# Third stage of an adaLN block: the gated residual by transpositions of VectorE's columns instead of products with diagonals

## The reference

```python
h = _layernorm(x) * (1 + ca) + sa
x = x + ga * _L1_attn_ref(h, ...)          # the change is here
# _L1_attn_ref, one step from a zero state:
xi = x @ W_in.T                            # x is h here
nr = B_real * xi ; ni = B_imag * xi        # the old state is zero
y  = sum(C_real * nr - C_imag * ni)        # so y is xi times a constant per feature
out = y @ W_out.T
return h + _rmsnorm(out, norm_w)           # the residual is h, so ga * h is needed too
```

## Time and profile before

| | us |
| --- | --- |
| three runs | 1878.19, 1873.54, 1880.81 (median 1878.19) |
| profiled execution | 1875.54 |
| its span | 1873.8 |
| stage C, first product to the first of stage D | 1237.61 to 1317.89 |
| `back`, last expert product to the first of stage C | 1205.6 to 1237.6 |

### The profile page before, as it was taken

One profiled execution on the slowest core, in us unless ns is written; L12 is line 12 of the kernel. 1 busy time (PEld: TensorE's weight loads), 2 busy tenths in 40 slices (PEclk: granted clock), 3 DMA queues, 4 the chain that ended last, 5 costly groups with the idle time before them and its releaser, 6 DMA issues.

```text
span 1873.8 us, 25682 instructions
## 1 busy us (share of the span) xinstructions
PE 1787.5 (95%) x8308; PEld 1401.4 (75%) x8308; DVE 1173.4 (63%) x2140; ACT 757.9 (40%) x1478; POOL 723.7 (39%) x698
## 2 busy tenths in 40 slices
PE   8889999999999999998898998979999999999998
PEld 5567878788878888876666776658778788787886
DVE  5557666676666766676754443557646657567476
ACT  2544555555454555534532222356632222213211
POOL 1433121211222211264344456635455536436342
PEclk9999999999999999999899999989999999999999
DMA  6101454535462544632368999730011001001001
GB/s 253 68 8 35 147 169 135 152 87 187 112 200 69 174 140 146 186 105 92 113 226 253 282 286 282 163 118 18 28 35 51 12 29 51 29 10 56 7 29 73
DMA packets 99955, 216.35 MB, mean 115 GB/s; under 512 B 8504, under 2 KB 33096, under 8 KB 98336
## 3 DMA queue, kind: packets, MB, share of 16 engines
q1 hardware_dynamic: 77744, 166.60, 28.1%
q0 software_dynamic: 11520, 28.96, 6.4%
q10 hardware_dynamic: 10608, 19.74, 3.2%
HBM read 123.93 MB, written 91.35 MB: 115 GB/s over the span
## 4 chain that ended last, share of the span: by engine, by line
PE 73%; DVE 9%; DMA 6%; issue 5%; POOL 3%; ACT 3%; POOLq 0%; ACTq 0%; DVEq 0%; SPq 0%
PE bank L810 21%; PE bank L812 20%; PE bank L811 20%; DMA u_d<-yt,sm 5%; PE bank L1051 3%; PE bank L1217 2%; PE bank L997 2%; PE bank L914 1%; DVE hh L2345 1%; DVE rr L2009 1%; PE bank L1058 1%; POOL gbt L2601 1%; PE bank L999 1%; POOL mark L2612 1%; PE bank L884 1%
## 5 line engine op out<-in xcount | busy, mean ns | idle before, releaser
L2009 DVE RECIPROCAL rr<-rr 128x256 f32<-128x256 f32 x128 | 218.8, 1730 | 0.0
L2444 POOL TENSOR_TENSOR x<-x,tmp 128x512 f32<-128x512 f32 x76 | 116.2, 1533 | 258.8 <-DVE tmp L2002 258.8
L810 PE MATMUL bank<-W1a,hT 128*128 128x512 f32 x512 | 209.4, 409 | 3.4 <-DVE hT L1931 3.4
L810 PE MATMUL bank<-hT,W1b 128*128 128x512 f32 x512 | 208.8, 408 | 2.4 <-DVE hh L2302 2.4
L811 PE MATMUL bank<-hT,W1b 128*128 128x512 f32 x512 | 204.0, 398 | 0.0
L812 PE MATMUL bank<-hT,W1b 128*128 128x512 f32 x512 | 203.8, 398 | 0.0
L812 PE MATMUL bank<-W1a,hT 128*128 128x512 f32 x512 | 201.1, 393 | 0.0
L811 PE MATMUL bank<-W1a,hT 128*128 128x512 f32 x512 | 200.3, 391 | 0.0
L2302 DVE TENSOR_TENSOR hh<-hh,bank 128x512 f32<-128x512 f32 x64 | 43.8, 688 | 183.4 <-PE bank L812 146.7
L2369 POOL TENSOR_TENSOR W<-stage,W 128x1024 fp32r<-128x1024 f32 x32 | 77.2, 2412 | 184.4 <-ACT W L1300 182.1
L2034 DVE SCALAR_TENSOR_TENSOR kt<-bank,kt 128x256 fp32r<-128x256 f32 x128 | 50.5, 395 | 152.8 <-ACT vt L1439 152.6
(11 more groups left out here) (299 smaller groups left out, 4555.3 us busy)
## 6 DMA issues: line engine op xcount, KB each, us to landing
hs_d<-bor SPq DMA_DIRECT2D x24, 1548.0 KB, 12.0
ws_d<-W SPq DMA_DIRECT2D x48, 512.0 KB, 6.1
WB<-ws_d SPq DMA_DIRECT2D x8, 3072.0 KB
stage<-wa SPq DMA_DIRECT2D x32, 512.0 KB, 5.5
stage<-wbe SPq DMA_DIRECT2D x24, 512.0 KB, 4.2
stage<-wdn SPq DMA_DIRECT2D x24, 512.0 KB, 3.9
hg<-hs_d ACTq DMA_DIRECT2D x39, 258.0 KB
mw<-wmod SPq DMA_DIRECT2D x5, 1024.0 KB, 5.0
```

The lines of the kernel that those rows point to most:

```text
L810: pe.matmul(o, lhs(HI), rhs(HI), start=start, stop=False, **kw)
L2009: dve.reciprocal(rr[:, pair, h], rr[:, pair, h]).then_inc(r_rec, 1)
L2444: pool.tensor_tensor(xt, xt, tmp[:, (key + t) % 2, :], ALU.add).then_inc(ring_done, 1)
```

## The change

The diagonals are gone. DVE multiplies each chunk in `tmp` by its gate, feature by feature, while the features still lie on partitions (`gated_columns`, 16 instructions, into `gh`, which takes the place of `dg`). PE then turns the four chunks of a tile by four transpositions (fp32, 128x128) at the end of the tile, and the result goes to x as before. The wait for the bank of this result moves from the tile's start to its end. ACT may write a chunk into `tmp` only when DVE has read the chunk two before it. The rows of layernorm (2, 1) are scaled by DVE (`normed_rows`) and not by ACT, ahead of the statistics of (2, 2). `normed` of a batch runs for all four tiles before the first `gated` of the next.

```diff
-        def over_diag(a):
-            return a("before_dg", [P, 8208]), a("dg", [P, NB, 2, NC, P], F32R)
+        def over_gated(a):
+            return a("before_gh", [P, 8208]), a("gh", [P, 2, NC, S])
@@ PE, step_c
-                pe.wait_ge(dg_lo, NC * (b + 1))
...
-                    if n < 2:
-                        pe.wait_ge(ring_read, ln_at(2, 0, 2 + (n + RING[("ln", 2, 0, 1)]) % 2) + 1)
-                    else:
-                        pe.wait_ge(res_read, n - 1)
...
-                            gated = pe.matmul(o[:, c * P:(c + 1) * P], h(wl), dg[:, b, wr, c, :],
-                                              start=at_ends[0], stop=at_ends[1], skip_group_check=True)
                         if c == NC - 1:
                             product.then_inc(y_full, 1)
+                            if n < 2:
+                                pe.wait_ge(ring_read, ln_at(2, 0, 2 + (n + RING[("ln", 2, 0, 1)]) % 2) + 1)
+                            else:
+                                pe.wait_ge(res_read, n - 1)
+                            for i in range(NC):
+                                if t == 0:
+                                    pe.wait_ge(gh_done, NC * b + i + 1)
+                                gated = pe.transpose(o[:, i * P:(i + 1) * P], gh[:, b % 2, i, t * P:(t + 1) * P], ident[:, :])
                             gated.then_inc(res_full, 1)
@@ ACT, ln_out_chunk and back
+                if k == 2 and (b, c) >= (0, 2) or (k, b) == (3, 0) and c < 2:
+                    act.wait_ge(gh_done, ((k - 2) * NB + b) * NC + c - 1)
...
-                for b in range(NB):
-                    for c in range(NC):
-                        act.activation(dg[:, b, HI, c, :], ident[:, :], ACT.Copy, scale=gcol[:, c, b:b + 1]) \
-                            .then_inc(dg_hi, 1)
...
-                ln_scaled(2, 1)
@@ DVE
-            def diagonals():
-                for b in range(NB):
-                    for c in range(NC):
-                        dve.wait_ge(dg_hi, b * NC + c + 1)
-                        dve.scalar_tensor_tensor(out=dg[:, b, LO, c, :], ...).then_inc(dg_lo, 1)
+            def normed_rows(k, b):
+                dve.wait_ge(c_scaled, (k - 2) * NB + b + 1)
+                dve.wait_ge(xn_ready, ln_index(k, b))
+                col = column((k, b))
+                for t in range(NT):
+                    last = dve.tensor_scalar(xn_of(k, b)[:, t, :], x[:, b * NT + t, :], crs[:, col + t:col + t + 1],
+                                             cnm[:, col + t:col + t + 1], ALU.mult, ALU.add)
+                last.then_inc(xn_ready, 1)
+            def gated_columns(b, c):
+                n = ln_at(2, b, c)
+                if b == 0 and c == 0:
+                    dve.wait_ge(gcol_full, 16 * NB)
+                if b >= 2 and c == 0:
+                    dve.wait_ge(res_full, NT * (b - 1))
+                dve.wait_ge(ring_read, n + 1)
+                dve.tensor_scalar(gh[:, b % 2, c, :], tmp[:, n % 2, :], gcol[:, c, b:b + 1], None, ALU.mult) \
+                    .then_inc(gh_done, 1)
             def back():
-                diagonals()
                 c_stats(2, 0)
                 c_scales((2, 0))
                 c_stats(2, 1)
                 c_scales((2, 1))
+                normed_rows(2, 1)
+                for c in range(NC):
+                    gated_columns(0, c)
@@ DVE, step_c: gated_columns(b + 1, t) behind each gated(b, t), for b < 3
-                normed(b - 1, (0, 1))
+                normed(b - 1, range(NT))
                 gated(b, 0)
-                normed(b - 1, (2, 3))
+                if b < 3:
+                    gated_columns(b + 1, 0)
                 add_normed(b - 1, 2)
                 gated(b, 1)
```

More of the change, by code:

```diff
@@ L324, in over_h1 @@
             return a("before_h1", [P, 6144]), a("h1", [P, NT, HP])
-        def over_diag(a):
-            return a("before_dg", [P, 8208]), a("dg", [P, NB, 2, NC, P], F32R)
+        def over_gated(a):
+            return a("before_gh", [P, 8208]), a("gh", [P, 2, NC, S])
         (hT, hF, (hg, hts, sgs, pps, at, tab, sm), (_, mst), (_, lw), (_, WB), (W1a, W2, _, W1b), (_, xw), (_, mw, prow), (_, x0),
-         (_, h1), (_, dg)) = shared(
+         (_, h1), (_, gh)) = shared(
             [lambda a: a("hT", [P, 2, NC, NB * S], F32R), lambda a: a("hF", [P, NC, NB * S]), over_hT, over_lo, over_late,
              over_both,
-             *map(second, (weights, over_w2, over_mods, over_x0, over_h1, over_diag))])
+             *map(second, (weights, over_w2, over_mods, over_x0, over_h1, over_gated))])
         hold = sb("hold", [P, 16384 + 12304])
@@ L476, in build @@
         gcol_full = sem("gate_columns_full")
-        dg_hi = sem("gate_diagonals_hi")
-        dg_lo = sem("gate_diagonals_lo")
+        gh_done = sem("c_columns_gated")
         c_scaled = sem("c_ln_scales_done")
@@ L1582, in back @@
                 split_d(0, 1)
-                act.wait_ge(gcol_full, 16 * NB)
-                for b in range(NB):
-                    for c in range(NC):
-                        act.activation(dg[:, b, HI, c, :], ident[:, :], ACT.Copy, scale=gcol[:, c, b:b + 1]) \
-                            .then_inc(dg_hi, 1)
-                    if b < 3:
-                        late_row(b)
+                for b in range(3):
+                    late_row(b)
                 late_modc(0)
@@ L2170, in slots @@
                 weighted(SLOTS - 1)
-            def diagonals():
-                for b in range(NB):
-                    for c in range(NC):
-                        dve.wait_ge(dg_hi, b * NC + c + 1)
-                        dve.scalar_tensor_tensor(out=dg[:, b, LO, c, :], in0=ident[:, :], scalar=gcol[:, c, b:b + 1],
-                                                 in1=dg[:, b, HI, c, :].bitcast(F32), op0=ALU.mult,
-                                                 op1=ALU.subtract).then_inc(dg_lo, 1)
+            def normed_rows(k, b):
[15 more added lines that the diff above has]
+                    .then_inc(gh_done, 1)
             def c_stats(k, b):
@@ L2253, in step_c @@
                     gated(0, 0)
+                    gated_columns(1, 0)
                     c_stats(2, 3)
                     gated(0, 1)
+                    gated_columns(1, 1)
                     c_scales((2, 2), (2, 3))
                     gated(0, 2)
+                    gated_columns(1, 2)
                     gated(0, 3)
+                    gated_columns(1, 3)
                     return
                 c_scales(*([(3, b - 2)] if b > 1 else []), ("y", b - 1))
-                normed(b - 1, (0, 1))
+                normed(b - 1, range(NT))
                 gated(b, 0)
-                normed(b - 1, (2, 3))
+                if b < 3:
+                    gated_columns(b + 1, 0)
                 add_normed(b - 1, 2)
                 gated(b, 1)
+                if b < 3:
+                    gated_columns(b + 1, 1)
                 add_normed(b - 1, 3)
@@ L2268, in step_c @@
                 gated(b, 2)
+                if b < 3:
+                    gated_columns(b + 1, 2)
                 gated(b, 3)
+                if b < 3:
+                    gated_columns(b + 1, 3)
             def step_d(g, b):
```

## The result

| | before | after |
| --- | --- | --- |
| median of 17 runs | 1877.55 us | 1872.28 us |
| profiled span | 1873.8 us | 1868.7 us |
| PE busy in the span | 1787.5 us | 1785.2 us |

The ratio is 0.9978, with a 95% interval of 0.9968 to 0.9988: 4.1 us faster (2.3 to 6.0), where 9.3 were forecast. The sign is as forecast, the gain is less than half.

The account below looks back on a forecast made before the run. PE's own instructions were taken to bound stage C; -14.6 us of PE work plus waits of 0.5, 0.8, 3.0, 0.5 and 0.5 gave -9.3, so 1867.5 us from a mean of 1877.0, range 1861 to 1876.

Parts of the forecast that it names:

- Products out, transpositions in: PE in stage C: dropping diagonal products saves 21.8 us, 64 transpositions cost 7.2, so PE's own sum is -14.6.
- What DVE adds: `gated_columns` on DVE: 0.53 us each until its result, 0.46 of DVE's time; with four row scalings 9.2 us more.
- Batch 2: Stage C, ahead of tile 9: PE waits 3.0 us more for `normed`, behind `late_gate` and POOL's adds.
- The clock: PE's clock in stage C: comes back where it does now, about 1246, with no cost counted for a fall.
- the slower rival: Stall at `gated_columns(1, 3)` grows to 6.5 us or more and PE's clock falls, 7.5 more: +4.7, 1881.5 us; chance 0.06.
- its own disproof: Forecast wrong if PE's `gh` group waits over 2 us for DVE, stage C's clock falls, or tile 9 doesn't wait.
- DVE stands behind POOL's runs: Less gain: `gated_columns(1, 3)` meets `late_gate`, PE's first group of batch 1 stands 5 us: -4.8, 1872 us; chance 0.19.
- Start of stage C: PE gains 1 to 2 us, gives it back at chunks 2 and 3: 0.5 worse; bounds 1.5 better, 2.5 worse.
- Batch 1: Stage C's batch 1: `gated_columns` may wait for POOL's `late_gate`, 0.5 us of new waiting.
- Batch 3: Stage C's batch 3: DVE's scales queue behind `gated_columns`, some 0.8 us of new waiting for PE.
- Stage D: Its first product waits for the last low part, which shows more with shorter tiles: 0.5 us.
- the rival of more gain: DVE and POOL don't hinder each other over `gh`: -12.3, 1864.5 us, or 1862 with two waits fewer; chance 0.21.

Follow-up runs that it names:

- gate_early: The changed kernel with POOL's `late_gate` moved from behind stage C's first batch to ahead of that batch's low parts: 1864.33 us, ratio 0.9938 to the kernel before.
- psum_cols: The changed kernel with `gated_columns` reading PE's PSUM bank instead of `tmp`, using pre-gated scale and shift, and DVE's order changed: 1869.94 us, ratio 0.9968 to before.
- normed_split: The changed kernel with `normed` split again, two before the batch's first `gated` and two after, as in the kernel before: 1871.16 us, ratio 0.9969 to before.
- act_rows: The changed kernel with the rows of layernorm (2, 1) scaled by ACT again instead of DVE: 1874.46 us, ratio 0.9989 to the kernel before.
- gate_early_again: gate_early run a second time, on the chip of two other runs: 1866.02 us, ratio 0.9939 to the kernel before.

## Why the prediction came out wrong in size

- **Products out, transpositions in: held.** The tile was 3.67 for a forecast 3.6. PE's own work in stage C fell by 13.3 in gate_early, where the clock stayed up from tile 1 on (75.56 to 62.26), against the forecast 14.6. That transpositions are cheap in a row, on which the weighing against the Trainium skill's 275 ns (there for bf16, here fp32) rested, held too: 0.36 for four. Whether transpositions keep the clock up no run here tests.
- **What DVE adds: 0.48 each, not 0.53**, and up to 1.26 beside POOL, but for the 6.43. The price held.
- **Batch 2 was the step that failed.** To compare instants, 1.4 us are added to those of after, by which its statistics began sooner. `late_gate` began at 1257.2, forecast 1257.1; POOL's adds ended at 1270.0, forecast 1271.5. But DVE came to the statistics only at 1273.4, since the gated chunk ahead of them, which the prediction had at 0.46 and as done before POOL's adds, stood for 6.43. From there on it took 9.1 for a forecast 8.7, and `normed` was through at 1282.5 in place of 1280.2. That the wait ahead of tile 9 came out as forecast, 3.82 for 3 to 4, is luck, because PE was late as well: the same stall held back the next layernorm's rows, 2.49 ahead of tile 8, for which the prediction had nothing. So 6.3 us at two tiles in place of the 1.22 of before: 5.1 new for a forecast 3.0.
- **The clock: its term was nothing, and it fell.** Only the slower rival had it fall, by a stall of 6.5 us or more. It fell some 2.2 us into the wait of 3.82 (with 2.49 one tile before) and was at 0.50 from 1280 to 1286, and tile 9 cost 2.4 more. This is what the prediction named as its own disproof, with the rival's price of 7.5 for it too high.
- **The rival "DVE stands behind POOL's runs" is what happened, one batch later.** It was placed at `gated_columns(1, 3)`, beside `late_gate` itself. That one took 1.26, and stood beside the low part just ahead of `late_gate`:

```profile
1254.52 1.27 POOL L2391 TENSOR_TENSOR hT<-tmp,hT 128x512 fp32r<-128x512 f32 x1 [2.99 <-ACT hT L1354]
```

```profile
1254.80 1.26 DVE L2186 TENSOR_SCALAR gh<-tmp,gcol 128x512 f32<-128x512 f32 x1
```

Among `late_gate`'s instructions of 4x512, which follow each other with 0.08 us and more between them, DVE gets through: the first gated chunk of batch 2 took 0.48 there, at 1262.23. It is the 128x512 run queued up behind `late_gate` that shuts it out. The rival's 1872 is the time that was measured, in part by luck: it had one wait of 5 us and no fall of the clock. The profile before had shown it: the 5.55 lay beside just this run. I read it as belonging to `late_gate`.
- **Start of stage C:** forecast 0.5 worse. The first product comes 2.1 sooner and tile 0 waits 2.87 in place of 1.14, so together 0.3 better. Within its bounds. **Batch 1**: 1.62 for 1.08, 0.5 as forecast, but not by the path named: PE waited for ACT's second pair of rows (1254.91 to 1256.42), and `late_gate` began only at 1255.75. **Batch 3**: 0.34 and 0.29 for 0.40, 0.2 new for a forecast 0.8; the prediction's own terms (4.6 against 3.6 plus 0.4) give 0.6. **Stage D**: 1.06 for 0.89, 0.2 for 0.5.

Two of the prediction's sums are off by little: the rival of more gain is -9.3 less 0.5, 0.5 and 1.5, so -11.8 and not -12.3, and the forecast is 1877.0 less 9.3, so 1867.7 and not 1867.5.

In sum, by the profiles: own work 1.3 less gained than forecast, clock 2.4, batch 2 another 2.1, against 1.7 less lost at the start, in batch 3 and at D. That is 4.1 of the 4.5 us between the forecast -9.3 and the profiled -4.8. That what `late_gate` backs up on POOL is the cause, and not DVE's load, is shown: with `late_gate` moved and every DVE instruction kept, some 7 us come back and stage C takes 70.6, the 71 of the forecast. That it works by shutting DVE out is read from the traces (6.43, and in psum_cols 5.94 at the next instruction with both sources in SBUF). How the 7 us divide between that and POOL's late adds isn't measured.

The Trainium skill (SBUF — State Buffer, Who interferes with whom) has the exclusion for a whole instruction for a tensor_scalar in a two-port mode too. The prediction cited it as untested. The traces agree for `gated_columns`, though none says which mode it runs in, and show it for several instructions in a row: 6.43 and 6.41.

## What to carry to other kernels

When work is added to an engine, look in the trace for an instruction of it that once took many times its usual duration, and see what ran beside it. If it was another engine's run without a gap, the new instruction may land there, and it will have more behind it than the old one had. Moving what backs that run up (here 9 us of small work, put ahead of the stage) can be worth more than the change itself, and nothing without it: here nothing in all in the kernel before and some 7 us in the changed one. Look at what it then lies beside, too: here it took back 0.9 to 2.0 us ahead of the stage.

## What the runs showed of the hardware

- A DVE instruction with its sources in SBUF took 6.43 (the changed kernel), 6.41 (normed_split) and 5.94 us (psum_cols) beside five 128x512 instructions of POOL that followed each other without a gap. A gated chunk took 0.48 where it started ahead of them by 1.0 us (1269.56 and 1270.57 in act_rows). With its source in PSUM and one more operation the chunk took 0.79 to 0.81 in all 16 cases of psum_cols, beside single instructions of POOL.
- Beside POOL's instructions of 4x512 DVE was held for less than the length of one: an `add_normed` took 1.78 for 0.68 (1262.62, the changed kernel), an instruction of 128x4 took 1.22 for 0.16 beside a TENSOR_TENSOR of 1.25 (1228.97 in gate_early_again).
- PE's clock was at 0.50 before the end of an idle time of 3.82 us and still 1.00 at the end of 2.49. In tile 0 it was at 0.50 after 2.87: three products took 1.59 us from 1238.59. It also fell after PE had resumed, about 1 us after a wait of 2.32 (act_rows) and 1.4 us after one of 3.33 (psum_cols). So the length of the last wait alone didn't tell whether it would fall.
